# Storing the turned fp16 parts of the adjacency matrix and loading them as they are for the last layer

## The chip, the cores and the metric

One core of one Trainium2 chip runs the whole program. The metric is device time in microseconds (us) of one launch. The kernel before the change takes 728.18 us, the median of three runs (727.69 to 729.91). The profiled execution of the same kernel took 727.12 us; the span that its trace shows, from the first instruction to the last, is 724.8 us.

## The reference, cut to what matters

Four graph layers in a row work on x (2048 x 256) and one dense matrix adj (2048 x 2048, float32). Every layer normalizes x, applies a ReLU, computes a term and adds it to x; the last layer takes x's sign instead of a weighted product:

```python
h = relu(layernorm(x)); x = x + (D^-1/2 adj.T D^-1/2) @ (h @ W0) + b0      # layer 0
h = relu(layernorm(x)); inc = adj + head(adj > 0)                         # layer 1
x = x + (inc @ h) / sum(inc)
h = relu(layernorm(x)); ht = (h @ W2) in 4 heads of 256                    # layer 2
e = leaky_relu(src_i + dst_j) + adj;  x = x + mean_heads(softmax(e) @ ht)
h = relu(layernorm(x)); xw = max(sign(h), 0) @ sign(W3).T                  # layer 3
x = x + relu(adj @ xw)
```

So adj is used four times: transposed in layer 0, as rows in layer 1 (with a small number added to the positive entries), as the additive term of the attention in layer 2, and as it is in layer 3. Since the tensor engine contracts over the partitions, layers 1 to 3 need adj (or a matrix made from it) with the contracted index on the partitions, which is the transposed matrix for rows loaded as they are.

## The kernel before, in words

Rows come in 16 blocks of 128 (NB = 16), a quarter (`q`) is four of them, and every float32 operand of the tensor engine is split into two fp16 parts, a high part (the value rounded) and a low part (what is left). adj times 256 is split while it is loaded; the parts stay on chip for layer 0 and are written once to `nat_dram` (fp16, high and low).

**Turning.** Layers 2 and 3 need the transposed adj. `turn_adj(n)` (SP, L383) loads a 512 x 512 tile of one part from `nat_dram` with a transposing DMA, two DMAs for the two parts, into one of two slots (`turn_l1` for the first four tiles, `turn_l2` for the other twelve). There are 16 tiles, four (`g`) to a quarter. GpSimd's queue then writes the tile to `adjt_dram` as float32: `widen_high(n)` (L545) writes the high part, converted, and `add_low(n)` (L549) adds the low part in memory. SP may turn tile n into its slot again when tile n-2 has been widened (semaphores `wide`).

**SP's queue** does all loads in one written order. During layer 1: `load_rows(t)` (L365) brings block t of adj, 1 MB, for the sign and count on ScalarE (L1003, L1007), which leads to the row that VectorE fills (`fill`, L1346) and that the tensor engine transposes (L699). In that order stand tiles 0 and 1 after the load of block 11, then the loads of blocks 12 to 15, then tiles 2 and 3. Tiles 4 to 15 follow in layer 2, four ahead of each `load_e(q)` (L436): that loads quarter q of `adjt_dram` in four groups of four 256 KB DMAs, each group when its place in `e_in` is free (when VectorE has used it in the last head of the quarter before). ScalarE takes the exponential of it in place (`exp_adj`, L1044).

**Layer 2** has 16 groups (4 quarters x 4 heads) of 16 steps. A step: VectorE makes 128x512 numerators (L1473), ScalarE rounds them to the high part (L1168), VectorE takes the low part (L1480), the tensor engine does 12 matmuls (L835 to L837). Four slots lie between VectorE and the tensor engine. After every group ScalarE scales the head's result (L1098) and GpSimd's queue adds it to x (L586).

**Layer 3** needs the transposed adj in fp16 parts once more, all 16 blocks: the tile `at3` has eight places of 8 KB per partition. The float32 rows are loaded from `adjt_dram` (L458, L463), ScalarE rounds them (`at3_high`, L1156), VectorE takes the low part (`at3_low`, L1528): blocks 0 and 1 in quarters of a block inside heads 2 and 3 of the last quarter, block 2 partly at their end, the others after the heads. The tensor engine does 32 matmuls for each block (L877, L878), the first four blocks partly before `xw` is complete; VectorE adds the result to x (`layer3_out`, L1562) and SP stores it (L472).

Of the kernel before, what the change touches and what calls it, by code (L numbers as in the profile page):

```python
# [28 lines left out]
P = 128  # L29
# [10 lines left out]
def gnn_stack(nc, x_d, adj_d, w0_d, b0_d, w2_d, a2_d, w3_d, out_d):  # L40
# [21 lines left out]
    adjt_dram = nc.dram_tensor("adj_t", (NB, P, N), F32, kind="Internal").ap()  # L62
    u_dram = nc.dram_tensor("u_rows", (NB, HEADS, P), F32, kind="Internal").ap()

    with ExitStack() as ctx:
# [120 lines left out]
        adjt_early = [view(RING3 + 8 * KB * (k + 1), [N], F32) for k in range(2)]  # L186
# [17 lines left out]

        def adjt_slot(i):
            if i < 2:
                return adjt_early[i].rearrange("p (g m) -> p g m", g=QB)
            g = TG * ((i - 2) % 4)
            return e_in[:, :, g:g + TG, :].rearrange("p r j n -> p r (j n)")
# [118 lines left out]
        adjt_in = [sem(f"adjt_in{k}") for k in range(6)]  # L328
        at3_hi_done = sem("at3_hi_done")
        at3_lo_done = sem("at3_lo_done")  # L330
# [12 lines left out]
        def _(sp):  # L343
# [117 lines left out]
            def load_adjt(i):  # L461
                k = (i - 2) % 4
                sp.dma_start(adjt_slot(i), adjt_dram[i].rearrange("p (g m) -> p g m", g=QB)  # L463
                             ).then_inc(adjt_in[k], 16)

            for k in range(4):
                sp.wait_ge(p_done, NQ * HEADS * NB - NB + TG * (k + 1))
                load_adjt(2 + k)
# [125 lines left out]
        def _(pe):  # L594
# [288 lines left out]
            pe.wait_ge(at3_lo_done, 2)  # L883
# [4 lines left out]
            pe.wait_ge(at3_lo_done, 3)  # L888
# [3 lines left out]
            pe.wait_ge(at3_lo_done, 4)  # L892
# [6 lines left out]
            for i in range(4, NB):  # L899
                pe.wait_ge(at3_lo_done, i + 1)  # L900
# [5 lines left out]
        def _(act):  # L906
# [165 lines left out]
            for g in range(TG):  # L1072
                act.wait_ge(wide[g], 16)
            ht_high(0)
# [61 lines left out]
            def at3_high(i, part, parts=4):  # L1136
                k = (4 + i) % 8
                if part == 0:
                    if i < 2:
                        act.wait_ge(adjt_in[4 + i], 16)  # L1140
                        if i == 1:
                            act.wait_ge(at3_lo_done, 1)
                    else:
                        act.wait_ge(adjt_in[(i - 2) % 4], 16 * ((i - 2) // 4 + 1))
                    if i == 2:
                        act.wait_ge(at3_lo_done, 2)
                    if i == 3:
                        act.wait_ge(head_added, 16 * (NQ * HEADS - 1))
                        act.wait_ge(xw_done, 2 * (NQ - 1))
                    if i >= 8:  # L1150
                        act.wait_ge(o_ps, i - 7)
                high = at3[:, k, 0, :, :].rearrange("p (g j) n -> p g (j n)", g=QB)
                source = adjt_slot(i)
                if parts > 1:
                    high, source = high[:, part, :], source[:, part, :]
                ins = nc.scalar.activation(high, source, copy)  # L1156
                if part == parts - 1:
                    ins.then_inc(at3_hi_done, 1)

            def head_high(q, hp, b, first, norms=False, turns=False):  # L1160
                head = 2 * hp + b
                group = q * HEADS + head
                for j in range(EARLY if first else 0, NB):
# [38 lines left out]
            at3_high(3, 0, 1)  # L1202
# [8 lines left out]
            for i in range(4, NB):  # L1211
                at3_high(i, 0, 1)
# [3 lines left out]
        def _(dve):  # L1216
# [246 lines left out]
            for g in range(TG):  # L1463
                dve.wait_ge(wide[g], 16)
            vp_cols = vp_j[:, :, :].rearrange("p t h -> p h t")
# [53 lines left out]
            def at3_low(i, part, parts=4):  # L1519
                k = (4 + i) % 8  # L1520
                if part == 0:
# [75 lines left out]
```

## Time and profile before

| | value |
|---|---|
| median of 3 runs | 728.18 us (727.69 to 729.91) |
| profiled execution | 727.12 us, span of the trace 724.8 us |
| TensorE (PE) busy | 691.0 us, 95% of the span |
| VectorE (DVE) busy | 629.4 us, 87% |
| ScalarE (ACT) busy | 472.4 us, 65% |
| GpSimd (POOL) busy | 135.6 us, 19% |
| share of the 16 DMA engines, SP's queue (q1) | 53.7%, 117.10 MB |
| share of the 16 DMA engines, GpSimd's queue (q0) | 25.4%, 41.42 MB |
| layer 2's products, one step | 12 matmuls |
| granted clock | 0.995 of 2.4 GHz in the mean |

Busy time is the time in which an engine works on at least one instruction; DMA-issuing instructions of SP do not count as busy. A DMA's time "to landing" runs from its issue to the last update of its semaphore. In a stretch where both queues are active the DMA share can be above 1, since it adds the times that packets took. Times within the trace count from the span's start: layer 0 ends near 170, layer 1 near 274, the heads of layer 2 run from about 316 to 662, and layer 3 ends at 722.

### The profile page before, as it was taken

The numbers are of one execution on the slowest core, as the hardware profiler recorded it, in microseconds if no ns is written. First come the engines' busy times: TensorE is split into PE (matmuls) and PEld (weight loads), VectorE is DVE, ScalarE is ACT, GpSimd is POOL, SyncE is SP. The second block draws the span as 40 slices with busy tenths as digits, with TensorE's granted clock in tenths as the row PEclk, the third lists the DMA queues.
The fourth block names the chain that finished last, engine by engine and source line by source line (L and its number), as shares of the span: only waits on it lengthen the run. The fifth ranks groups of instructions, "written<-read, shape, count | busy, mean of one in ns | idle before, by whom it ended". The sixth has DMA issues, their size and how long they took to land.

```text
span 724.8 us, 16131 instructions
## 1 busy us (share of the span) xinstructions
PE 691.0 (95%) x6480; PEld 586.1 (81%) x6480; DVE 629.4 (87%) x1161; ACT 472.4 (65%) x814; POOL 135.6 (19%) x162
## 2 busy tenths in 40 slices
PE   3998999986999999999999999999999999999998
PEld 3676888875888885468888888888888888888887
DVE  6898579688999854799999999989999899998683
ACT  3887153648887624886557867578766778667660
POOL 3962721301223220001210021200121000000000
PEclk9999999998999999999999999999999999999999
DMA  9997999677499887759988779997999831126791
GB/s 337 342 318 238 426 424 309 201 185 219 134 275 277 190 175 234 162 127 243 235 193 235 176 166 257 199 267 161 229 224 228 267 129 30 30 81 188 255 392 46
DMA packets 146457, 159.54 MB, mean 220 GB/s; under 512 B 90896, under 2 KB 103888, under 8 KB 141904
## 3 DMA queue, kind: packets, MB, share of 16 engines
q1 hardware_dynamic: 127328, 117.10, 53.7%
q0 software_dynamic: 19056, 41.42, 25.4%
q8 instruction: 52, 0.85, 0.5%
q14 instruction: 21, 0.17, 0.1%
HBM read 76.15 MB, written 52.46 MB: 177 GB/s over the span
## 4 chain that ended last, share of the span: by engine, by line
PE 60%; DVE 21%; ACT 6%; DMA 4%; issue 4%; SPq 2%; POOL 2%; ACTq 0%; DVEq 0%; POOLq 0%
PE ps L835 11%; PE ps L837 11%; PE ps L836 11%; DVE arena L1473 6%; PE ps L775 6%; DVE arena L1480 5%; PE ps L877 4%; PE ps L878 4%; DVE arena L1346 2%; DMA arena<-in_adj_dram 2%; SPq L383 2%; ACT arena L1003 2%; PE ps L719 2%; PE ps L721 1%; PE ps L720 1%
## 5 line engine op out<-in xcount | busy, mean ns | idle before, releaser
L835 PE MATMUL ps<-arena 128*128 128x257 f16 x1024 | 279.9, 273 | 1.0 <-DVE arena L1480 0.6
L837 PE MATMUL ps<-arena 128*128 128x257 f16 x1024 | 279.4, 273 | 0.0
L836 PE MATMUL ps<-arena 128*128 128x257 f16 x1024 | 279.2, 273 | 0.0
L1168 ACT ACTIVATE arena<-arena 128x512 f16<-128x512 f32 x252 | 158.3, 628 | 93.8 <-PE ps L837 56.3
L1473 DVE SCALAR_TENSOR_TENSOR arena<-arena,w_j 128x512 f32<-128x512 f32 x256 | 190.2, 744 | 0.0
L1480 DVE TENSOR_TENSOR arena<-arena 128x512 f16<-128x512 f32 x256 | 175.7, 687 | 8.1 <-ACT arena L1168 7.8
L835 PEld LDWEIGHTS ps<-arena 128*128 128x128 f16 x1024 | 99.9, 98 | 15.0 <-issue 1.4
L836 PEld LDWEIGHTS ps<-arena 128*128 128x128 f16 x1024 | 100.3, 98 | 12.5
L837 PEld LDWEIGHTS ps<-arena 128*128 128x128 f16 x1024 | 99.8, 97 | 12.9
L719 PE MATMUL ps<-arena 128*128 128x257 f16 x256 | 71.1, 278 | 1.9 <-DVE arena L1298 1.9
L721 PE MATMUL ps<-arena 128*128 128x257 f16 x256 | 70.5, 275 | 0.0
L720 PE MATMUL ps<-arena 128*128 128x256 f16 x256 | 70.1, 274 | 0.0
L670 PE MATMUL ps<-arena 128*128 128x256 f16 x224 | 61.1, 273 | 0.0
L671 PE MATMUL ps<-arena 128*128 128x256 f16 x224 | 61.1, 273 | 0.0
L672 PE MATMUL ps<-arena 128*128 128x256 f16 x224 | 61.1, 273 | 0.0
L877 PE MATMUL ps<-arena 128*128 128x256 f16 x256 | 56.2, 273 | 0.9 <-DVE x L1562 0.9
L878 PE MATMUL ps<-arena 128*128 128x256 f16 x256 | 56.2, 273 | 0.0
L1044 ACT ACTIVATE arena<-arena,amax 128x512 f32<-128x512 f32 x64 | 45.4, 710 | 6.8 <-DMA arena<-adj_t 6.8
L586 POOL DMA_DIRECT2D x<-arena x15 | 14.0, 934 | 185.0 <-ACT arena L1098 185.0
L1528 DVE TENSOR_TENSOR arena<-arena 128x2048 f16<-128x2048 f32 (+1 forms) x22 | 37.4, 1705 | 9.5 <-ACT arena L1156 9.5
L957 ACT ACTIVATE arena<-arena,rstd 128x256 f16<-128x256 f32 x16 | 8.1, 508 | 54.2 <-POOL rstd L520 54.2
L1249 DVE SCALAR_TENSOR_TENSOR arena<-arena 128x1024 f16<-128x1024 f32 x32 | 38.7, 1228 | 5.0 <-ACT arena L912 4.3
(154 smaller groups left out, 1154.9 us busy)
## 6 DMA issues: line engine op xcount, KB each, us to landing
adj_t<-arena POOLq DMA_DIRECT2D x32, 1024.0 KB, 7.9
arena<-in_adj_dram SPq DMA_DIRECT2D x32, 512.0 KB, 6.0
arena<-in_adj_dram SPq DMA_DIRECT2D x16, 1024.0 KB, 5.8
adj_parts<-arena SPq DMA_DIRECT2D x16, 1024.0 KB, 25.7
arena<-adj_t SPq DMA_DIRECT2D x64, 256.0 KB, 4.5
arena<-adj_t SPq DMA_DIRECT2D x16, 1024.0 KB, 6.7
x<-arena POOLq DMA_DIRECT2D x15, 512.0 KB, 5.7
arena<-u_rows SPq DMA_DIRECT2D x4, 1024.0 KB, 14.7
```

The costliest lines, as they stand in the source:

```text
L670: mm(ps[:, bank, 0:D], nat[:, t, 0, j, :], g_hi[:, j, :], start=(j == 0), stop=False)
L719: mm(ps[:, bank, 0:DE], parts[:, 0, j, :], h1_hi[:, j, 0:DE], start=s, stop=False)
L720: mm(ps[:, bank, 0:D], parts[:, 0, j, :], h1_lo[:, j, :], start=False, stop=False)
L721: ins = mm(ps[:, bank, 0:DE], parts[:, 1, j, :], h1_hi[:, j, 0:DE], start=False, stop=e)
L835: mm(ps[:, bank, 0:DE], hi, ht_hi[:, head, j, 0:DE], start=s, stop=False)
L836: mm(ps[:, bank, 0:DE], hi, ht_lo[:, head, j, 0:DE], start=False, stop=False)
L837: ins = mm(ps[:, bank, 0:DE], lo, ht_hi[:, head, j, 0:DE], start=False, stop=e)
L877: mm(ps[:, bank, 0:D], at3[:, k, 0, j, :], xw[:, j, :], start=(j == 0), stop=False)
L878: ins = mm(ps[:, bank, 0:D], at3[:, k, 1, j, :], xw[:, j, :], start=False, stop=(j == NB - 1))
L1168: nc.scalar.activation(p_hi[:, j % 4, :], prob[:, j % 4, :], copy).then_inc(p_hi_done, 1)
L1473: v.scalar_tensor_tensor(prob[:, j % 4, :].rearrange("p (r n) -> p r n", r=QB), u_bc[:, h, q * (QB * P):(q + 1) * (QB * P)].rearrange("p ( ...
L1480: v.tensor_tensor(p_lo[:, j % 4, :], prob[:, j % 4, :], p_hi[:, j % 4, :], ALU.subtract).then_inc(p_lo_done, 1)
```

## The change

Each turned tile, high and low part, is also written to a new DRAM tensor `at16_dram` (fp16, 16 MB) by SP: `store_turned(n)`, one DMA of 1 MB in pieces of 1 KB. Layer 3's blocks are loaded from it straight into `at3`, 1 MB each in rows of 8 KB, and the tensor engine waits on their landing. The loads of float32 rows for layer 3, the 16 roundings on ScalarE and the 16 subtractions on VectorE go, those within the last heads too. A slot is turned again when its tile was both widened and stored; ScalarE and VectorE, before they write where the first four tiles stood, wait for their stores too. GpSimd's code is the same.

```diff
+    at16_dram = nc.dram_tensor("adj_t_parts", (NB, P, 2, N), F16, kind="Internal").ap()
...
             def turn_adj(n):
                 q, g = n // TG, n % TG
                 if n >= 2:
+                    sp.wait_ge(stored[n % 2], 16 * (n // 2))
                     sp.wait_ge(wide[(n - 2) % TG], 16 * ((n - 2) // TG + 1))
...
+            def store_turned(n):
+                q, g = n // TG, n % TG
+                slot = (turn_l1 if q == 0 else turn_l2)[n % 2]
+                sp.wait_ge(turned[n % 2], 32 * (n // 2 + 1))
+                sp.dma_start(at16_dram[QB * q:QB * (q + 1), :, :, TG * P * g:TG * P * (g + 1)
+                                       ].rearrange("r p a m -> p a r m"), slot).then_inc(stored[n % 2], 16)
...
             for n in range(2):
                 sp.wait_ge(inc_in[4 - n], 32)
                 turn_adj(n)
+            for n in range(2):
+                store_turned(n)
             for t in range(12, NB):
                 reload_rows(t)
             for n in range(2, QB):
                 turn_adj(n)
+            for n in range(2, QB):
+                store_turned(n)
...
             sp.wait_ge(ht_ps, 2 * NB)
+            def load_parts(i):
+                k = (4 + i) % 8
+                sp.dma_start(at3[:, k, :, :, :].rearrange("p a j n -> p a (j n)"), at16_dram[i]).then_inc(at3_in[k], 16)
+
             for q in range(1, NQ):
                 for g in range(TG):
                     turn_adj(QB * q + g)
+                    if g >= 1:
+                        store_turned(QB * q + g - 1)
+                store_turned(QB * q + TG - 1)
                 load_e(q)
-            for i in range(2):
-                sp.dma_start(adjt_early[i], adjt_dram[i]).then_inc(adjt_in[4 + i], 16)
...
+            for b in range(2):
+                sp.wait_ge(stored[b], 16 * (NB // 2))
+            for i in range(3):
+                load_parts(i)
+            for h in range(HEADS - 1):
+                sp.wait_ge(p_done, ((NQ - 1) * HEADS + h + 1) * NB)
+                load_parts(QB + h)
+            sp.wait_ge(head_added, 16 * (NQ * HEADS - 1))
+            sp.wait_ge(xw_done, 2 * (NQ - 1))
+            load_parts(3)
+            sp.wait_ge(p_done, NQ * HEADS * NB)
+            load_parts(7)
...
-            for i in range(6, NB):
-                sp.wait_ge(at3_lo_done, i - 3)
-                load_adjt(i)
-                if i >= 8:
-                    store_out(i - 8)
+            for i in range(8, NB):
+                sp.wait_ge(o_ps, i - 7)
+                load_parts(i)
+                store_out(i - 8)
...
             def layer3_products(i, blocks):
                 k, bank = (4 + i) % 8, 4 + i % 4
+                pe.wait_ge(at3_in[k], 16 * (i // 8 + 1))
...
             for g in range(TG):
                 act.wait_ge(wide[g], 16)
+            for b in range(2):
+                act.wait_ge(stored[b], 32)
...
-                    if q == NQ - 1 and head >= 2 and j < 4:
-                        at3_high(head - 2, j)
-                    if q == NQ - 1 and head == HEADS - 1 and j >= 12:
-                        at3_high(2, j - 12)
...
-                        if q == NQ - 1 and h >= 2 and 4 <= j < 8:
-                            at3_low(h - 2, j - 4)
...
-            at3_low(2, 0, 1)
-            at3_low(3, 0, 1)
-            for i in range(4, NB):
-                at3_low(i, 0, 1)
-                layer3_out(i - 4)
-            for t in range(NB - 4, NB):
+            for t in range(NB):
                 layer3_out(t)
```

## Rows read from the trace of the kernel before

**Rows 1.** The page's chain that ended last, by line: share of the span.
```profile
PE ps L835 11%; PE ps L837 11%; PE ps L836 11%; DVE arena L1473 6%; PE ps L775 6%; DVE arena L1480 5%; PE ps L877 4%; PE ps L878 4%; DVE arena L1346 2%; DMA arena<-in_adj_dram 2%; SPq L383 2%; ACT arena L1003 2%; PE ps L719 2%; PE ps L721 1%; PE ps L720 1%
```

**Rows 2.** Groups by line, the removed work: count, busy us, mean ns, idle before.
```profile
L1156 ACT ACTIVATE arena<-arena 128x2048 f16<-128x2048 f32 (+1 forms) x25 | 31.8, 1286 | 10.4 <-DMA arena<-adj_t 10.4
L1528 DVE TENSOR_TENSOR arena<-arena 128x2048 f16<-128x2048 f32 (+1 forms) x22 | 37.4, 1705 | 9.5 <-ACT arena L1156 9.5
```

**Rows 3.** Waits of PE, 600 to 690 us: for whom, total us, times, longest.
```profile
PE ps L877 <- DVE x L1562: 0.9, 1, 0.9
PE ps L853 <- ACT arena L1098: 0.4, 1, 0.4
PE ps L835 <- ACT arena L1168: 0.4, 1, 0.4
```

**Rows 4.** Order of time of SP's queue in layer 1: start us, us, line, DMAs.
```profile
206.38 19.22 SPq L365 DMA_DIRECT2D arena<-in_adj_dram  x4
228.00 16.48 SPq L383 DMA_TRANSPOSE arena<-adj_parts  x4
274.14 9.50 SPq L436 DMA_DIRECT2D arena<-adj_t  x16
```

**Rows 5.** Single issues: tile 1's last transpose, then block 12's load, each to landing.
```profile
L383 SPq DMA_TRANSPOSE arena<-adj_parts x1: 2309/2309/2309, 204.0 to 204.0; - x1
...
DMA to landing us min/median/max: 5.0/5.0/5.0
...
L365 SPq DMA_DIRECT2D arena<-in_adj_dram x1: 581/581/581, 206.4 to 206.4; - x1
...
DMA to landing us min/median/max: 6.2/6.2/6.2
```

**Rows 6.** Order of time behind block 12's landing, on ScalarE, VectorE, PE.
```profile
212.61 1.91 ACT L1003 ACTIVATE arena<-arena 128x2048 f16<-128x2048 f32 x1 [1.18 <-DMA arena<-in_adj_dram]
215.03 0.69 DVE L1352 SCALAR_TENSOR_TENSOR arena<-ps,arena 128x512 f16<-128x512 f32 x1 [1.04 <-ACT arena L992]
218.04 0.33 PE L699 MATMUL ps<-ident,arena 128*128 128x128 f32 x1 [0.29 <-DVE arena L1346]
```

**Rows 7.** Price of 1 MB: four 512 B broadcasts of 1 MB, then four 256 KB loads.
```profile
L448 SPq DMA_DIRECT2D arena<-u_rows x4: 379/3829/7026, 290.8 to 300.9; - x4
...
DMA to landing us min/median/max: 9.5/14.7/16.7
...
L436 SPq DMA_DIRECT2D arena<-adj_t x4: 337/432/436, 382.4 to 383.7; - x4
...
DMA to landing us min/median/max: 3.3/3.9/4.3
```

**Rows 8.** Busy us by stretch: PE, PEld, DVE, ACT, POOL, clock, DMA share, GB/s.
```profile
162.40:168.90 6.50, 0.00 (x0) 0.00 (x0) 5.57 (x10) 6.47 (x5) 1.30 (x3) 0.88 1.01 273
169.00:174.10 5.10, 5.10 (x24) 4.08 (x25) 3.97 (x18) 5.10 (x7) 1.37 (x3) 0.50 0.81 247
174.20:179.00 4.80, 4.80 (x47) 4.39 (x46) 4.23 (x5) 2.81 (x6) 0.00 (x0) 1.00 0.18 29
```

**Rows 9.** Quarter 2's first load_e group, from 468.2 us, and who waited for it.
```profile
L436 SPq DMA_DIRECT2D arena<-adj_t x4: 320/432/452, 468.2 to 469.6; - x4
...
  ACT arena L1044: 2.8, 1
...
DMA to landing us min/median/max: 4.4/8.3/9.3
```

**Rows 10.** Waits of PE, 465 to 580 us; then a stretch as in rows 8.
```profile
PE ps L835 <- DVE arena L1480: 0.6, 2, 0.4
440.00:450.00 10.00, 10.00 (x93) 8.87 (x92) 9.92 (x18) 7.01 (x17) 2.07 (x2) 1.00 1.23 262
```

**Rows 11.** Tile 11's two transposes in SP's queue, 452 to 461 us.
```profile
L383 SPq DMA_TRANSPOSE arena<-adj_parts x2: 2122/2273/2424, 450.2 to 452.7; - x2
...
DMA to landing us min/median/max: 4.7/6.1/7.5
```

More of the change, by code:

```diff
@@ L185, in gnn_stack @@
         turn_l2 = [view(RING3 + off, [2, QB, TG * P], F16) for off in (8 * KB, 16 * KB)]
-        adjt_early = [view(RING3 + 8 * KB * (k + 1), [N], F32) for k in range(2)]
         COUNTS = (1, 2, 9, 10, 11)
@@ L202, in gnn_stack @@
         HT_RING = 7
[L205 to L209, printed above, removed]
         H0_BANK = (0, 1, 6)
@@ L327, in gnn_stack @@
         ba_done = sem("ba_done")
-        adjt_in = [sem(f"adjt_in{k}") for k in range(6)]
-        at3_hi_done = sem("at3_hi_done")
-        at3_lo_done = sem("at3_lo_done")
+        at3_in = [sem(f"at3_in{k}") for k in range(8)]
+        stored = [sem(f"stored{b}") for b in range(2)]
         ba_t_ps = sem("ba_t_ps")
@@ L455, in _ @@
                     turn_adj(QB * q + g)
+                    if g >= 1:
+                        store_turned(QB * q + g - 1)
+                store_turned(QB * q + TG - 1)
                 load_e(q)
-            for i in range(2):
-                sp.dma_start(adjt_early[i], adjt_dram[i]).then_inc(adjt_in[4 + i], 16)
[L461 to L468, printed above, removed]
+            for b in range(2):
[10 more added lines that the diff above has]
+            load_parts(7)
             def store_out(t):
@@ L882, in _ @@
             pe.wait_ge(head_scaled, (NQ * HEADS - 1) * QB)
-            pe.wait_ge(at3_lo_done, 2)
             layer3_products(0, range(NB - QB))
@@ L887, in _ @@
             binary_turn(NQ - 1, 0, 0, ba_tail)
-            pe.wait_ge(at3_lo_done, 3)
             layer3_products(2, range(NB - QB))
@@ L891, in _ @@
             binary_product(NQ - 1, 0, 2, bat_tail)
-            pe.wait_ge(at3_lo_done, 4)
             layer3_products(3, range(NB - 2 * QB))
@@ L899, in _ @@
             for i in range(4, NB):
-                pe.wait_ge(at3_lo_done, i + 1)
                 pe.wait_ge(o_done, i - 3)
@@ L1134, in binary_out @@
                                      ps[:, bank + pair, :], copy, scale=1.0 / ADJ_SCALE).then_inc(xw_done, 1)
[L1136 to L1158, printed above, removed]
             def head_high(q, hp, b, first, norms=False, turns=False):
@@ L1201, in _ @@
                                   turns=(hp == 1 and b == 0))
-            at3_high(3, 0, 1)
             for r in range(QB):
@@ L1210, in _ @@
                 binary_out(NQ - 1, pair)
-            for i in range(4, NB):
-                at3_high(i, 0, 1)
         @block.vector
@@ L1464, in _ @@
                 dve.wait_ge(wide[g], 16)
+            for b in range(2):
+                dve.wait_ge(stored[b], 32)
             vp_cols = vp_j[:, :, :].rearrange("p t h -> p h t")
@@ L1517, in head_inverse @@
                 v.reciprocal(inv_l[:, b, :], inv_l[:, b, :]).then_inc(inv_done, 1)
-            def at3_low(i, part, parts=4):
-                k = (4 + i) % 8
-                if part == 0:
-                    dve.wait_ge(at3_hi_done, i + 1)
-                high = at3[:, k, 0, :, :].rearrange("p (g j) n -> p g (j n)", g=QB)
-                low = at3[:, k, 1, :, :].rearrange("p (g j) n -> p g (j n)", g=QB)
-                source = adjt_slot(i)
-                if parts > 1:
-                    high, low, source = high[:, part, :], low[:, part, :], source[:, part, :]
-                ins = v.tensor_tensor(low, source, high, ALU.subtract)
-                if part == parts - 1:
-                    ins.then_inc(at3_lo_done, 1)
             def quarter(q, first):
@@ L1563, in layer3_out @@
                                        ).then_inc(o_done, 1)
-            at3_low(2, 0, 1)
-            at3_low(3, 0, 1)
-            for i in range(4, NB):
-                at3_low(i, 0, 1)
-                layer3_out(i - 4)
-            for t in range(NB - 4, NB):
+            for t in range(NB):
                 layer3_out(t)
```

## The prediction

> **What bounds the kernel now.** I read the chain of waits first. It is mostly matmuls: lines 835 to 837 alone are a third of the span, and VectorE's two instructions of a step (L1473, L1480) come next [rows 1]. The work that the change removes, the splitting of L1156 and L1528, is not among its largest lines, although it is 31.8 us of ScalarE and 37.4 us of VectorE [rows 2]. So the next view is who made the tensor engine wait where that work stands: between 600 and 690 us, 0.9 + 0.4 + 0.4 us in all [rows 3]. That is what there is to win: the rest of the removed work lies beside matmuls that run without a gap.
>
> Then I read SP's queue, since the change adds to it. In layer 1 its order is on the chain: the load of block 12 is issued at 206.38, right behind the transposes of tiles 0 and 1, and the issues of blocks 13 to 15 follow it until 225.6 [rows 4]. It lands 6.2 us later [rows 5], at 212.6, and ScalarE, which had waited 1.18 us for it, starts at 212.61; VectorE, waiting 1.04 us for ScalarE, follows at 215.03; and the tensor engine, 0.29 us idle, at 218.04 [rows 6]. Each waits for the one before it, so this landing has no slack left.
>
> Last I read the loads of the next quarter (`load_e`). ScalarE waited 2.8 us for the first group of quarter 2 [rows 9], the tensor engine 0.6 us in two waits at the ends of quarters 1 and 2 [rows 10]: the four slots between VectorE and the tensor engine just cover the delay, and any more is the tensor engine's.
>
> **What the change removes.** All 25 instructions of L1156 and 22 of L1528 [rows 2]. The waits that they may cause are the three of rows 3. The 0.9 us (VectorE's addition of block 0 stands behind a subtraction) goes for certain; of the two of 0.4 us in the heads I take both. What is late next there is the tensor engine itself. Gain 1.7 us; bounds 0.9 and 1.7. Loads of layer 3 stay sixteen of 1 MB; eight have a place before the products need them, and the later ones are asked for seven blocks ahead, so I cost them at nothing. If that cover is gone, one late landing costs at most the 6.2 us of a 1 MB load [rows 5].
>
> **What one store costs.** Sixteen DMAs of 1 MB in 1 KB pieces; no row shows such a store. Two kinds of load bound it. Four broadcasts of 1 MB in 512 B pieces: the first is issued at 290.8, and the last at 300.9, landing 14.7 us later (the median; its own landing lies near it), so 24.8 us for four, 6.2 us each. Four loads of 256 KB in 2 KB pieces: the first lands at 382.4 + 3.3, the last at 383.7 + 4.3, so 2.3 us for three, 3.1 us for 1 MB [rows 7]. 1 KB lies between; I take 4 us, and 3.1 and 6.2 as the ends.
>
> The Trainium skill ("DMA: Bandwidth & Descriptors", section Specifications) puts the line rate at 435 GB/s for pieces from 512 B on; an estimate from that page is 2.4 us for a store, and the sum below would be 3 us smaller. The trace disagrees for 512 B, with its 6.2 us [rows 7], so I stay with the rows.
>
> **Layer 1: stores 0 and 1 move block 12's load.** SP's order becomes transposes, wait for tile 0, store 0, wait for tile 1, store 1, and only then the loads of blocks 12 to 15. Waiting in SP's queue holds all four. Tile 1's last transpose is issued at 204.0 and lands 5.0 us later, at 209.0 [rows 5]; store 1 can't be issued before, so block 12's load goes out at 209.7 at the earliest (one issue of 0.58 us behind it [rows 5]), 3.3 us late. That is the lower end, with stores that delay nothing. But the load stands behind 2 MB on the same queue. Of its 6.2 us to landing 3.1 are transfer (as four 256 KB loads take), and I give half of the rest, 1.6, to the way from the last byte to the semaphore. So tile 1's bytes are through at 207.4; two stores take 8 us, to 215.4; the load itself 3.1, to 218.5; the message 1.6, to 220.1; and GpSimd's `widen_high(0)`, which falls into this stretch, takes engines from it, by my estimate 1.2 us of its own 4. It lands at 221.3 instead of 212.6: 8.7 us late. By rows 6 there is no slack, so the tensor engine stops 8.7 us more before block 11's transposes. With 6.2 us a store it would be 13 us, and 16 with all 4 us of GpSimd's: the upper end. None of it comes back: the rest of the layer waits for this engine or for the same chain behind it, shifted alike.
>
> Such a stop has one precedent. The tensor engine did nothing from 162.4 to 168.9; after that the granted clock stood at 0.50 (1.2 of 2.4 GHz), with 24 matmuls in 5.1 us where 47 went in 4.8 us at full clock [rows 8]. At the full rate 24 take 2.5 us, so 2.6 us were lost. A stop of 9 us behind steady work should repeat that: 2.5 us more. Bounds 0 (no fall) and 3.5.
>
> Stores 2 and 3 stand behind the last transposes of the layer, issued from 228.0 to 244.5; the next thing in SP's queue, `load_e`, is at 274.1 [rows 4]. ScalarE's and VectorE's new wait for these four stores comes later still, so 30 us cover it; price nothing, and if the cover were gone, one store's 4 us.
>
> **Layer 2: twelve more stores.** `turn_adj`'s new wait for store n-2 stands beside the wait for the same tile's widening, two DMAs one after the other, and ends before it; nothing for that. But the DMA engines are full: a share of 1.23 at 440 to 450 us [rows 10]. In quarter 1, tile 10's transposes are followed by store 9, tile 11's by store 10, and store 11 waits for tile 11, whose last transpose is issued at 452.7 and lands at about 460.2 [rows 11]. `load_e` is due at 468.2 and now stands behind what is left of stores 10 and 11. Stores 9 and 10 compete with GpSimd's writes on which tile 11 waits, so tile 11 comes some 3 us later, store 11 goes out at 463, and with half of the engines its 4 us take 8, to 471: `load_e`'s first group, last landing at 469.6 + 9.3 = 478.9 [rows 9], is some 3 us later. The reserve is used up [rows 10], so that is the tensor engine's loss. The same arrangement of stores 13 to 15 stands ahead of quarter 3's `load_e`: 3 us again. Quarter 1's own loads landed after 4.3 us at most [rows 7] with no wait behind them; stores 5 to 7 I cost at nothing, the reserve covering one 4 us delay. Together 6 us. Bounds: 0 (the stores are through before 468) and 8 us a boundary (stores 10 and 11 whole ahead of the load), 16.
>
> **The sum**, on the profiled execution's 727.12 us (span 724.8 and 2.3 around it): 727.1 - 1.7 + 8.7 + 2.5 + 6 = 742.6. That execution is 1.1 us below the median shown, so against the median it is 743.7; I say 743.
>
> **Rivals.**
> 1. Only layer 1 pays; layer 2's stores are through before `load_e` is due. For it: between tile 11's landing at 460.2 and 468.2 stand 8 us [rows 9, 11], enough for two stores at full rate. Against: the full engines of rows 10. 727.1 - 1.7 + 8.7 + 2.5 = 736.6, on the median 737.7.
> 2. Cheap stores: 3.1 us or less each, no clock fall, no loss in layer 2. Block 12 is then 3.3 to 6 us late: 727.1 - 1.7 + 3.3 to 6 = 728.7 to 731.4, on the median about 730 to 732.5.
> 3. Heavy stores, 6.2 us: 13 in layer 1, 3 for the clock, 10 to 14 in layer 2: 751.5 to 755.5, on the median 753 to 757.
> 4. Not slower: the splitting gone from the last heads and layer 3 is the whole effect, because block 12's load overtakes. That needs it to land by 214.3, 1.7 us later than now, where SP can't issue it before 209.7: it would have to land in 4.6 us instead of 6.2, through two stores. 725.4 to 727, median 726.5 to 728. Decided by that landing.
>
> The Trainium skill ("DMA: Bandwidth & Descriptors", Queues, rings and completion order) says that descriptors of one queue are taken up in ring order but may finish out of it; by that rule the load's data stand behind both stores', as in my sum; served in another order, the fourth case would come nearer. No row here shows a load behind a store.
>
> **Chances and range.** Forecast (738 to 749) 0.45; only layer 1 (734 to 738) 0.22; cheap stores (729 to 734) 0.15; heavy 0.10; not slower 0.08. The likeliest is 743. From 731 to 754 holds some 85%, with a little of the second and third case left out. A measurement of this kernel can tell 0.3%, 2.2 us, from no change. Faster than 726 takes the fourth case at its best: 0.04; within 0.3% (726 to 730.4) the rest of it and the cheapest stores: 0.07; slower 0.89.
>
> **What would show it.** Right: SP's queue shows stores between tile 1's transposes and block 12's load, which lands near 221; PE idles some 9 us before L699 near 218 and its clock stands at 0.50 after it; the waits of L1044 for `adj_t` grow to some 6 us at both quarters' ends; the three waits of rows 3 are gone. Wrong: block 12 lands by 216; the waits at the quarters' ends stay near 2.8 us; or the tensor engine waits elsewhere, on `at3` loads in layer 3 for instance.

## The result and the profile after

The changed kernel takes 749.1 us (median of 4 runs, 745.98 to 753.64) against 727.93 us (727.41 to 729.91) of the kernel before on the same chip: ratio 1.029, 95% interval 1.023 to 1.035. Slower, as forecast, 6 us beyond the forecast of 743 and inside the range of 731 to 754. The profiled execution is the slowest of the four (753.64 us, span 751.8), so its stages below add up to some 6 us more than the medians differ by (27.0 against 21.2). Every trace shows one execution, and those of runs 3, 5 and 12 below are the fastest of theirs: sizes are compared between traces roughly, and the ratios decide.

First the page of the changed kernel: busy times, the granted clock by slice, SP's queue, one group of instructions.

```profile
PE 701.2 (93%) x6480; PEld 591.0 (79%) x6480; DVE 593.2 (79%) x1139; ACT 442.0 (59%) x789; POOL 137.6 (18%) x162
...
PEclk9999999989989999999999999989999899999999
...
q1 hardware_dynamic: 138592, 133.87, 59.1%
...
L1052 ACT ACTIVATE arena<-arena,amax 128x512 f32<-128x512 f32 x64 | 45.5, 710 | 29.7 <-DMA arena<-adj_t 29.7
```

VectorE lost 36 us of work and ScalarE 30, as the diff says, SP's queue gained 16.8 MB, and the span grew by 27 us. The tensor engine issues the same matmuls and is busy 10 us longer: the clock has low slices it did not have. ScalarE's idle time ahead of `exp_adj` (now L1052) is 29.7 us; it was 6.8. In the chain that ended last DMAs now have 27% of the span; they had 4%.

Where the span grew, from the starts of the same instructions in both traces: layer 0 ends 1.6 us earlier (the diff does not touch it; two executions differ by so much), layer 1 costs 7.8 us, the ends of quarters 0, 1 and 2 cost 6.0, 8.4 and 8.6 us, and the tail, from the last head on, gives 2.2 back. -1.6 + 7.8 + 6.0 + 8.4 + 8.6 - 2.2 = 27.0, the difference of the spans.

**Layer 1.** SP's queue in order of time, to be held against [rows 4]:

```profile
192.98 11.90 SPq L377 DMA_TRANSPOSE arena<-adj_parts  x4
204.93 3.04 SPq L385 DMA_DIRECT2D adj_t_parts<-arena  x2
208.01 22.91 SPq L358 DMA_DIRECT2D arena<-in_adj_dram  x4
233.73 16.03 SPq L377 DMA_TRANSPOSE arena<-adj_parts  x4
```

The two stores stand ahead of block 12's load. Single issues, the stores and then that load, each to landing [rows 5]:

```profile
L385 SPq DMA_DIRECT2D adj_t_parts<-arena x2: 580/638/697, 204.9 to 207.4; - x2
...
DMA to landing us min/median/max: 5.1/5.7/6.2
...
L358 SPq DMA_DIRECT2D arena<-in_adj_dram x1: 738/738/738, 208.0 to 208.0; - x1
...
DMA to landing us min/median/max: 8.9/8.9/8.9
```

It goes out 1.6 us later and takes 8.9 us instead of 6.2: it lands at 216.9, 4.3 us later on the clock of the trace and 5.9 later measured from layer 0's end. The chain behind it on ScalarE and the tensor engine, in order of time [rows 6]:

```profile
216.97 1.91 ACT L1011 ACTIVATE arena<-arena 128x2048 f16<-128x2048 f32 x1 [7.13 <-DMA arena<-in_adj_dram]
...
219.91 0.20 PE L753 MATMUL ps<-wa_hi,arena 128*128 128x8 f16 x2 [3.87 <-ACT arena L991]
...
222.40 0.90 PE L710 MATMUL ps<-ident,arena 128*128 128x128 f32 x3 [2.19 <-DVE arena L1325]
```

The tensor engine's waits of the whole stretch, 205 to 280 us, for whom, total, times, longest, of after and then of before:

```profile
PE ps L753 <- ACT arena L991: 3.9, 1, 3.9
PE ps L710 <- DVE arena L1325: 3.3, 2, 2.2
```

```profile
PE ps L699 <- DVE arena L1346: 1.9, 2, 1.6
```

The waits grew from 1.9 to 7.2 us, 5.3 more. Then the stretches around the stop; columns as in [rows 8]:

```profile
213.00:220.00 7.00, 3.13 (x32) 2.58 (x31) 0.60 (x1) 3.03 (x4) 0.00 (x0) 1.00 1.39 384
220.50:227.20 6.70, 4.80 (x23) 3.83 (x24) 6.14 (x14) 5.23 (x7) 3.82 (x5) 0.50 0.67 174
227.40:234.00 6.60, 6.60 (x68) 6.01 (x67) 5.83 (x9) 4.70 (x9) 0.38 (x2) 1.00 1.25 309
```

After the stop the clock stands at 0.50: 23 matmuls in 4.8 busy us, where at the full clock of the next stretch 23 take 6.60 x 23 / 68 = 2.2. That is some 2.6 us more (an estimate: the two stretches do not hold the same mix of matmuls), and 5.3 + 2.6 = 7.9 agrees with the layer's 7.8.

**Layer 2, the end of quarter 1.** The tensor engine's waits between 380 and 610 us, the stretch of three quarters' ends (0.6 us in the last two before [rows 10], none in the first), and SP's queue in order of time:

```profile
PE ps L846 <- DVE arena L1461: 16.9, 4, 6.5
```

```profile
447.97 7.60 SPq L377 DMA_TRANSPOSE arena<-adj_parts  x2
455.61 0.59 SPq L385 DMA_DIRECT2D adj_t_parts<-arena  x1
469.56 10.70 SPq L377 DMA_TRANSPOSE arena<-adj_parts  x2
480.31 4.96 SPq L385 DMA_DIRECT2D adj_t_parts<-arena  x2
485.37 20.75 SPq L441 DMA_DIRECT2D arena<-adj_t  x16
```

After tile 10's transposes and store 9 SP issues nothing for 13 us. Store 9 by itself, then tile 11's transposes, then the first group of `load_e` [rows 9, 11]:

```profile
L385 SPq DMA_DIRECT2D adj_t_parts<-arena x1: 592/592/592, 455.6 to 455.6; - x1
...
DMA to landing us min/median/max: 13.9/13.9/13.9
...
L377 SPq DMA_TRANSPOSE arena<-adj_parts x2: 2386/5330/8275, 469.6 to 472.0; - x2
...
DMA to landing us min/median/max: 7.9/10.3/12.7
...
L441 SPq DMA_DIRECT2D arena<-adj_t x4: 614/1215/1277, 485.4 to 488.6; - x4
...
  ACT arena L1052: 8.3, 1
...
DMA to landing us min/median/max: 7.6/8.0/8.2
```

SP's waits in that stretch are for tile 9's widening (L374), then for store 9 (L377), then for tile 11's landing (L385). The chain of waits (start, us, what) runs over the last two of them to the load:

```profile
SPq L374 <- DMA adj_t<-arena: 8.6, 1, 8.6
SPq L377 <- DMA adj_t_parts<-arena: 4.7, 1, 4.7
SPq L385 <- DMA arena<-adj_parts: 3.8, 1, 3.8
```

```profile
455.61 13.93 DMA adj_t_parts<-arena
...
471.99 12.69 DMA arena<-adj_parts
...
488.58 7.88 DMA arena<-adj_t
```

Tile 11 may be turned when tile 9 is widened and stored. The widening is through 4.7 us before the store, at 464.8; the store, issued 455.6, lands at 469.5 and is the last. Tile 11 lands at 484.7, store 11 waits for it, and `load_e`, behind store 11 in the same queue, goes out at 485.4, although its place had been free since 480.4 (the end of the VectorE instruction that frees it; 468.2 in the trace before). Measured from that moment, tile 11 lands 12.3 us later than before: 2.4 us from the later widening, 4.8 from the wait for store 9, and 5.1 because its own transposes take 15.1 us from the first issue to the landing instead of 10.0 [rows 11]. The tensor engine then stops 5.83 us (order of time), and the clock falls once more (busy time by stretch): 24 matmuls in 5.1 us, then 58 in 6.2.

```profile
498.60 0.38 PE L846 MATMUL ps<-arena 128*128 128x257 f16 x1 [5.83 <-DVE arena L1461]
```

```profile
497.00:503.70 6.70, 5.10 (x24) 3.60 (x25) 5.94 (x10) 5.92 (x11) 0.95 (x2) 0.50 1.04 204
503.80:510.00 6.20, 6.20 (x58) 5.50 (x57) 4.37 (x7) 3.20 (x6) 0.00 (x0) 1.00 1.04 337
```

The same happens at the other two ends: stores 5 and 13 take 15.2 and 13.8 us to land, `load_e` goes out 3.7 and 6.9 us after its place is free, and the tensor engine is idle 4.4 and 6.5 us. At all three ends SP waits for the store when the widening is done, up to 7.7 us (its waits between 320 and 680 us):

```profile
SPq L377 <- DMA adj_t_parts<-arena: 16.8, 3, 7.7
```

From 610 to 752 us the view of waits lists none for the tensor engine: those of [rows 3] are gone and no load of layer 3 holds it.

### The profile page after: what moved, and what is told of

The parts are those of the page before. It is cut to its first block, busy times and chain, and to the rows that moved or that the text cites. A ratio compares the mean times of both kernels' runs of the same rounds, so it can differ in the third digit from the quotient of the medians.

```text
span 751.8 us, 16107 instructions
## 1 busy us (share of the span) xinstructions
PE 701.2 (93%) x6480; PEld 591.0 (79%) x6480; DVE 593.2 (79%) x1139; ACT 442.0 (59%) x789; POOL 137.6 (18%) x162
## 4 chain that ended last, share of the span: by engine, by line
PE 37%; DMA 27%; DVE 15%; ACT 6%; issue 5%; SPq 5%; POOL 4%; ACTq 0%; POOLq 0%; DVEq 0%
DMA adj_t<-arena 8%; DMA arena<-adj_parts 7%; DMA adj_t_parts<-arena 6%; PE ps L786 5%; PE ps L846 5%; PE ps L848 5%; PE ps L847 5%; DMA arena<-adj_t 4%; PE ps L889 4%; PE ps L890 4%; SPq L377 4%; DVE arena L1325 2%; DVE arena L1461 2%; DVE arena L1454 2%; DVE arena L1228 2%
## 5 line engine op out<-in xcount | busy, mean ns | idle before, releaser
L846 PE MATMUL ps<-arena 128*128 128x257 f16 x1024 | 282.9, 276 | 16.9 <-DVE arena L1461 16.9
L848 PE MATMUL ps<-arena 128*128 128x257 f16 x1024 | 282.4, 276 | 0.0
L847 PE MATMUL ps<-arena 128*128 128x257 f16 x1024 | 282.3, 276 | 0.0
L846 PEld LDWEIGHTS ps<-arena 128*128 128x128 f16 x1024 | 101.0, 99 | 32.1 <-ACT arena L1154 17.9
L848 PEld LDWEIGHTS ps<-arena 128*128 128x128 f16 x1024 | 100.9, 99 | 14.1
L847 PEld LDWEIGHTS ps<-arena 128*128 128x128 f16 x1024 | 101.3, 99 | 13.5
L730 PE MATMUL ps<-arena 128*128 128x257 f16 x256 | 72.5, 283 | 2.0 <-DVE arena L1277 2.0
L732 PE MATMUL ps<-arena 128*128 128x257 f16 x256 | 71.9, 281 | 0.0
L1052 ACT ACTIVATE arena<-arena,amax 128x512 f32<-128x512 f32 x64 | 45.5, 710 | 29.7 <-DMA arena<-adj_t 29.7
L1528 DVE SCALAR_TENSOR_TENSOR x<-ps,x 128x256 f32<-128x256 f32 x16 | 6.8, 424 | 48.8 <-PE ps L890 48.8
L597 POOL DMA_DIRECT2D x<-arena x15 | 16.8, 1117 | 146.5 <-ACT arena L1108 146.5
L786 PE MATMUL ps<-arena 128*128 128x512 f16 x192 | 42.5, 379 | 0.1
```

The lines of the kernel that those rows point to most:

```text
L730: mm(ps[:, bank, 0:DE], parts[:, 0, j, :], h1_hi[:, j, 0:DE], start=s, stop=False)
L732: ins = mm(ps[:, bank, 0:DE], parts[:, 1, j, :], h1_hi[:, j, 0:DE], start=False, stop=e)
L786: ins = mm(ps[:, k % HT_RING, :], h2_t[:, ha * DC + c, t * P:(t + 1) * P], wb[:, c, 512 * half:512 * half + 512], start=(n == 0), stop=(n ...
L846: mm(ps[:, bank, 0:DE], hi, ht_hi[:, head, j, 0:DE], start=s, stop=False)
L847: mm(ps[:, bank, 0:DE], hi, ht_lo[:, head, j, 0:DE], start=False, stop=False)
L848: ins = mm(ps[:, bank, 0:DE], lo, ht_hi[:, head, j, 0:DE], start=False, stop=e)
```

## The experiments

Runs 1 to 4 shared one chip, 5 to 8 a second, 9 to 11 the first again, run 12 had a third; each ratio is against the kernel before on the same chip, with its 95% interval. The medians of the kernel before beside them were 729.47, 729.27, 728.95 and 728.79 us. What a layer costs in a trace is counted as above, from the starts of the same instructions in the trace before.

**1. no_stores: the gain alone.**

```diff
-            for n in range(2):
-                store_turned(n)
...
-                sp.dma_start(at3[:, k, :, :, :].rearrange("p a j n -> p a (j n)"), at16_dram[i]).then_inc(at3_in[k], 16)
+                sp.dma_start(at3[:, k, :, :, :].rearrange("p a j n -> p a (j n)"), nat_dram[i * P:(i + 1) * P]).then_inc(at3_in[k], 16)
...
-                    if g >= 1:
-                        store_turned(QB * q + g - 1)
-                store_turned(QB * q + TG - 1)
```

> The changed kernel without any store of turned tiles and without the waits for them; layer 3's blocks are loaded from the split rows that are in memory already, in the same size and form (so the last layer's numbers are those of adj's rows as split, not turned). It has the gain of the change alone. Theory A (the loss comes from where the stores and their waits stand in SP's queue) and theory B (the loss is the DMA traffic that the stores add) both expect some 726 us, 1.7 to 2.2 less than before, no wait of the tensor engine at the quarters' ends beyond the 0.6 us of before, and none in layer 3. Were the new loads of layer 3 themselves at fault, it would be above 728.

All sixteen stores and every wait for them are left out. 725.13 us, ratio 0.995 (0.993 to 0.997). The removed splitting is worth some 2 us in the tail of the trace and half a per cent of the time (0.3 to 0.7), though it was 69 us of two engines' work. Layer 1, in which nothing is changed here, is 1.7 us longer than in the trace before: differences of that size between two traces say nothing. With the sixteen loads kept and only the stores gone, everything lost above is gone too: the loss belongs to the stores and what waits for them.

**2. layer1_stores: only stores 0 to 3.**

```diff
                 for g in range(TG):
                     turn_adj(QB * q + g)
-                    if g >= 1:
-                        store_turned(QB * q + g - 1)
-                store_turned(QB * q + TG - 1)
...
```

> As the one without stores, but tiles 0 to 3 are stored, in the changed kernel's order (tiles 4 to 15 are not stored, and layer 3 loads the split rows that are in memory). Both theories expect the layer 1 part of the loss and nothing at the quarters' ends: 726 + 6 to 9 = 732 to 735 us, block 12's load landing some 6 us later than before, a stop of the tensor engine of 6 us near 217 and one stretch of clock at 0.50 behind it. If the loss at the quarters' ends also shows, it does not come from the stores of layer 2.

Layer 3 loads what it loads in run 1. 732.83 us, 1.0049 (1.002 to 1.008): 7.7 us above run 1 on the same chip. Layer 1 lost 7.6 us in its trace, and the waits are nearly those of the changed kernel:

```profile
PE ps L708 <- DVE arena L1323: 3.3, 2, 2.2
PE ps L751 <- ACT arena L989: 3.2, 1, 3.2
...
PE ps L844 <- DVE arena L1459: 1.2, 2, 0.9
```

The last row is 380 to 610 us: 1.2 us where the changed kernel has 16.9. So layer 1's loss comes without layer 2's stores.

**3. rows_first: block 12's load ahead of the stores.**

```diff
-            for n in range(2):
-                store_turned(n)
             for t in range(12, NB):
                 reload_rows(t)
+            for n in range(2):
+                store_turned(n)
```

> The changed kernel with one move: the loads of blocks 12 to 15 stand ahead of stores 0 and 1 in SP's queue. Theory A: the whole layer 1 part goes, 8 us, to about 741 us; block 12 lands 6.2 us after its issue as before. Theory B: the same 2 MB are written in the same layer, the loads of blocks 14 and 15 and GpSimd's writes meet them, and half or more of the 8 us stays: 745 us or more.

749.27 us, 1.028 (1.024 to 1.032); the expected 741 was missed, and the time is that of the changed kernel. The load again lands after 6.6 us, at 212.8, and the stop at 217 is gone; yet layer 1 still loses 4.5 us in the trace, later. The waits of GpSimd's queue, 215 to 280 us, show where, and the landing of `widen_high(1)`, 10.3 us before:

```profile
POOL adj_t L560 <- DMA adj_t<-arena: 7.9, 2, 5.6
```

```profile
L556 POOL DMA_DIRECT2D adj_t<-arena x1: 1317/1317/1317, 221.0 to 221.0; - x1
...
DMA to landing us min/median/max: 12.7/12.7/12.7
```

The stores now run beside `widen_high(1)`; `add_low` waits 5.6 us for it in GpSimd's queue (3.2 before), with the row norms behind it that the next rows need. The tensor engine stops 1.4 us at 237 and 2.2 us at 243 (1.6 before). That the stores made `widen_high(1)` slower is likely but not shown by this run: it took 12.7 us in run 11 as well, where no store was issued before 242. Part of the cost had moved, and by time nothing was won.

The end of quarter 2 in this trace, where the order is that of the change, shows something else: `load_e` goes out 0.1 us after its place is free, and the end costs 6.3 us all the same. Stores 14 and 15 are on their way until 578 and 580, and the second group of loads takes up to 14.1 us, where it took up to 9.2 before:

```profile
L385 SPq DMA_DIRECT2D adj_t_parts<-arena x2: 580/586/593, 561.6 to 565.4; - x2
...
DMA to landing us min/median/max: 14.9/15.7/16.5
...
L441 SPq DMA_DIRECT2D arena<-adj_t x4: 320/432/432, 576.8 to 578.1; - x4
...
DMA to landing us min/median/max: 6.9/9.1/14.1
```

So loads that are issued in time can still land late behind stores, which is what the prediction had priced for these ends.

**4. reordered: run 3, and in layer 2 two stores early and two behind `load_e`.**

```diff
                 for g in range(TG):
+                    if g == 2:
+                        store_turned(QB * q)
+                        store_turned(QB * q + 1)
                     turn_adj(QB * q + g)
-                    if g >= 1:
-                        store_turned(QB * q + g - 1)
-                store_turned(QB * q + TG - 1)
                 load_e(q)
+                for g in range(2, TG):
+                    store_turned(QB * q + g)
```

> The changed kernel with all sixteen stores, in another order: blocks 12 to 15 ahead of stores 0 and 1; in each later quarter both first tiles stored before the third is turned (while GpSimd's queue still waits for a group's end), and the last two stored behind the next quarter's loads. No wait is taken out and no byte is saved. Theory A: nearly all of the loss goes, 726 to 730 us. Theory B: the same 16 MB still meet full DMA engines, and it stays above 735 us.

733.81 us, 1.0049 (1.001 to 1.008). Above the 726 to 730 expected: layer 1 costs 5 us (one stop of 4.4 us at 236 to 241; `widen_high(1)`, beside the two stores, takes 15.1 us). The quarters' ends are down from 23 us to 4.

**5. last_after: only the quarter's last store goes behind `load_e`.**

```diff
-                store_turned(QB * q + TG - 1)
                 load_e(q)
+                store_turned(QB * q + TG - 1)
```

> The changed kernel with one move: in each later quarter the last tile's store stands behind the next quarter's loads instead of ahead of them. Theory C (SP's queue: the loads go out late, because SP waits for the last tile ahead of them): the loads are issued when VectorE frees their places, as before, 5 us earlier than in the changed kernel at the end of quarter 1, and of the 6 to 8.6 us a boundary only 1 to 3 stay: 733 to 738 us. Theory D (the loads' own time to landing, among stores and GpSimd's writes): issue comes earlier but the landing stays where it was, 747 us or more.

744.76 us, 1.021 (1.013 to 1.028): the 733 to 738 of theory C were missed. In its trace `load_e` goes out 0.1, 1.2 and 0.1 us after its place is free, and the tensor engine is idle 0.5, 3.2 and 1.7 us there; but that trace is its fastest execution (737.96), and the median is not told apart from the changed kernel's second measurement (run 9). So it is not shown that moving the last store alone gains anything.

**6. second_early: the first two stores ahead of the third tile, all four ahead of `load_e`.**

```diff
+                    if g == 2:
+                        store_turned(QB * q)
+                        store_turned(QB * q + 1)
                     turn_adj(QB * q + g)
-                    if g >= 1:
-                        store_turned(QB * q + g - 1)
-                store_turned(QB * q + TG - 1)
+                for g in range(2, TG):
+                    store_turned(QB * q + g)
                 load_e(q)
```

> The changed kernel with one move: in each later quarter the second tile's store stands ahead of the third tile's transposes, so that it is written while GpSimd's queue waits, and the last tile's transposes no longer wait for it (they wait 15.2, 13.9 and 13.8 us for that store's landing now). The last store still stands ahead of the loads. Theory C: the last tile is turned some 6 to 8 us earlier, SP's wait for it ends before the loads are due, and 1 to 4 us a boundary stay: 734 to 741 us. Theory D: the last two stores still stand ahead of the loads in the same queue: 745 us or more.

739.95 us, 1.014 (1.009 to 1.020), within the 734 to 741 of theory C; the interval still touches that of run 9. All four stores still stand ahead of `load_e`, and it goes out in time all the same (0.1 us); the tensor engine is idle 0.8, 3.5 and 2.3 us, since the loads land late behind the stores: the second group of the middle end takes up to 11.8 us (8.6 before). The difference to the change is that the quarter's second store is issued ahead of its third tile's transposes, not behind them, so that the fourth tile, which waits for that store, is turned earlier.

**7. tiles_whole: the change with stores in pieces of 8 KB instead of 1 KB, loads in 1 KB.**

```diff
-    at16_dram = nc.dram_tensor("adj_t_parts", (NB, P, 2, N), F16, kind="Internal").ap()
+    at16_dram = nc.dram_tensor("adj_t_parts", (NB, P, 2, QB, TG * P), F16, kind="Internal").ap()
...
+                sp.dma_start(at16_dram[n], slot).then_inc(stored[n % 2], 16)
```

> The changed kernel with the same order and waits, but each tile is stored as one piece of 8 KB per partition (the loads of layer 3 read pieces of 1 KB instead, two DMAs a block). If the price of 1 KB pieces is what costs, a store lands earlier by 0.5 to 1 us of its 5 us alone, and the loss shrinks by 2 to 5 us, to 744 to 747. If place and waits in SP's queue cost, it stays within 2 us of the changed kernel, 747 to 751. Should layer 3 wait for its loads, that shows as waits of the tensor engine on them at the end.

740.64 us, 1.018 (1.011 to 1.025): below what either theory gave, but by the ratio not told apart from run 9 (1.021, 1.017 to 1.025). In its trace, with the order of the change untouched, `load_e` goes out in time (0.1 us), stores 5, 9 and 13 land after 10.1, 10.4 and 8.1 us, and the waits at the ends are 7.7 us, not 16.9. That the size of the pieces is part of a store's price is a reading of two traces; the times do not show it, and run 11 gains nothing from the same pieces.

**8. placed: reordered, and stores 0 and 1 wait until tile 1 is widened.**

```diff
             for t in range(12, NB):
                 reload_rows(t)
+            sp.wait_ge(wide[1], 16)
             for n in range(2):
                 store_turned(n)
```

> The reordered kernel with one wait more: stores 0 and 1 go out only when tile 1 is widened, so that they do not meet GpSimd's writes of tiles 0 and 1, on which GpSimd's queue and through it the row norms wait. If that meeting is what kept 4 to 5 us of layer 1's loss in both kernels with the rows first, the stop of 4.4 us near 236 goes and layer 1 loses 0 to 2: 727 to 731 us. If the DMA engines' fill as such is the cause, 733 us or more as the reordered one.

738.91 us, 1.016 (1.008 to 1.024): missed. The stop at 236 is gone; one of 4.6 us stands at 274 to 278, where `widen_high(3)`, beside stores 2 and 3, lands after 14.0 us (9.6 before), and tile 3 itself is turned late, behind stores 0 and 1.

**9. after_again: the changed kernel beside runs 10 and 11.**

> The changed kernel once more, unchanged, beside the next two: 1.02 to 1.03 times the kernel before, some 745 to 752 us. Its three later quarters' ends lose 6 to 9 us each again, and layer 1 some 8.

745.3 us, 1.021 (1.017 to 1.025), as expected. The size of the loss differs between the two measurements, 2.1 and 2.9%; its sign does not.

**10. placed_all: stores 2 and 3 wait for their own widening too.**

```diff
+            for g in range(2, TG):
+                sp.wait_ge(wide[g], 16)
             for n in range(2, QB):
                 store_turned(n)
```

> The placed kernel with one wait more: stores 2 and 3 go out only when tiles 2 and 3 are widened, at about 272 us, shortly ahead of the first loads of layer 2. If the meeting of stores with GpSimd's writes, on which the row norms wait, is what costs in layer 1, the stop of 4.6 us near 274 goes and layer 1 loses 0 to 2 us; with 1 to 2 us at two quarters' ends and the gain of some 2 us the time is 726 to 731 us, a ratio of 0.997 to 1.005. If the fill of the DMA engines costs wherever the stores stand, it stays at 733 or more.

733.99 us, 1.009 (1.006 to 1.012): missed, expected up to 1.005. The stop of 4.6 us stays, at 270 to 275. As in run 8, tiles 2 and 3 stand behind the postponed stores 0 and 1; they land 5 and 7 us later than in run 4, and GpSimd waits for its own writes (its queue, 240 to 282 us):

```profile
POOL adj_t L565 <- DMA adj_t<-arena: 14.4, 2, 8.5
```

**11. placed_all_whole: run 10 with run 7's pieces.**

> The same with each tile stored in pieces of 8 KB and layer 3's loads in pieces of 1 KB. If a cheaper store counts where the engines are full (as the kernel with whole tiles alone showed), another 0 to 2 us go at the quarters' ends: 724 to 730 us, 0.993 to 1.003 times the kernel before; layer 3 shows no wait on its loads, which then take longer. If not, it equals the one before it in this list within 1 us, or loses what layer 3's loads cost.

736.79 us, 1.009 (1.006 to 1.012): no better than run 10. The 724 to 730 of a cheaper store did not come.

**12. layer2_order: layer 1 as in the change, run 4's order in layer 2 alone.**

```diff
+                    if g == 2:
+                        store_turned(QB * q)
+                        store_turned(QB * q + 1)
                     turn_adj(QB * q + g)
-                    if g >= 1:
-                        store_turned(QB * q + g - 1)
-                store_turned(QB * q + TG - 1)
                 load_e(q)
+                for g in range(2, TG):
+                    store_turned(QB * q + g)
```

> The changed kernel with layer 1 left as it is, and layer 2's stores moved alone: the first two tiles of a quarter are stored before its third tile is turned, the last two behind the next quarter's loads; the same sixteen stores, bytes and waits. Theory C (late issue of the loads, from SP's waits): the loads are issued within 0.2 us of the moment when they are due at all three quarters' ends, the tensor engine stops 0 to 2.5 us at each instead of 4.5 to 6.5, and 1.006 to 1.013 times the kernel before, 733 to 738 us: layer 1's 7 to 8 us stay. Theory D (the stores' traffic): the loads are issued in time but land late all the same, and the ratio stays at 1.017 or more, 741 us and up.

736.04 us, 1.010 (1.006 to 1.014), as expected of the theory of late issue: `load_e` goes out 0.1 us after its place is free at all three ends. The waits of the tensor engine, 380 to 610 us and then 205 to 280 us:

```profile
PE ps L848 <- DVE arena L1463: 2.0, 2, 1.4
...
PE ps L755 <- ACT arena L993: 3.7, 1, 3.7
PE ps L712 <- DVE arena L1327: 3.3, 2, 2.2
```

Layer 1's stop is untouched, and the 16.9 us of the quarters' ends are 2.0. This trace is the fastest of seven executions and that of the change the slowest of four, but the times say the same: above run 2, which has no stores in layer 2, the change stood 1.6 to 2.4% and this run stands 0.5%. The store traffic is the same sixteen megabytes; only its order changed. So at the quarters' ends it is the order in SP's queue, not the amount of traffic, that costs most. No order that was tried beats the kernel before.

## Why the prediction was right and where it was wrong

**Gain, 1.7 us forecast.** The trace has 2.2, and run 1 has 0.3 to 0.7% of the time, 2 to 5 us. This was right: the splitting lay beside other work, and layer 3's loads cost nothing.

**Layer 1, 11.2 us forecast.** The trace has 7.8, and run 2 stands 7.7 above run 1. The mechanism is shown by runs 1 to 3: block 12's load behind two stores, ScalarE's wait for it, the stop, the clock at 0.50 behind it. The clock term was right (2.5 forecast, 2.6). The mis-sized term is the store, for which I took 4 us. SP's part came out as worked: the load was issued at 208.0, which is 209.6 on the clock of the trace before, and I had 209.7. But behind the two stores it took 8.9 us to land and not 11.6, so the 8.7 us late are 5.9. Of these the tensor engine lost 5.3.

The 2.4 us for a store that I had estimated from the 435 GB/s of the Trainium skill ("DMA: Bandwidth & Descriptors", Specifications) were nearer than my 4 us in this stretch, where the load lost only 2.7 us behind two stores, part of them done before it was issued; stores 5, 9 and 13 of layer 2, with 13.8 to 15.2 us to landing, are far from it. The Trainium skill's rule that one queue's descriptors are taken up in ring order (the same page, Queues, rings and completion order) agrees with this trace: the load did not overtake, and landed at 216.9, behind store 1 (207.4 + 6.2 = 213.6).

**Layer 2, 6 us forecast, the step that failed.** The trace has 23.0; by the ratios of the change (1.021 to 1.029) above run 2 (1.0049) it is 12 to 18 us. What was wrong, in order of weight:

The step that failed is the sentence "`turn_adj`'s new wait for store n-2 stands beside the wait for the same tile's widening ... and ends before it; nothing for that". The store ended after the widening at all three ends, 4.3 to 7.7 us after it, 4.7 at the end of quarter 1. I had priced a store by transfers with next to no write of GpSimd's beside them, 3.1 to 6.2 us [rows 7], and halved the engines for the last store alone; stores 5, 9 and 13, which ran beside GpSimd's writes, took 13.8 to 15.2 us. The transposes of the last tile, for which I had added nothing, took 5.1 us longer at the end of quarter 1. So the last tile landed 12.3 us later, not the 3 that I had given it, its store went out behind it, and `load_e` stood behind that store. Run 12 shows that this order is the cost: 2.0 us of waits instead of 16.9.

What I did forecast, loads that land late behind stores still on their way, is in the traces too, beside the late issue: it is what the end of quarter 2 in run 3 (6.3 us) and most of what is left at the ends in run 6 show. At 3 us an end it was priced too low.

The end of quarter 0, which I had "at nothing", cost 6 us, not far below the others. I read that its loads had landed after 4.3 us at most [rows 7], which is its first group alone, and took this for a reserve; the same queue with the same last tile stands ahead of them: they go out 3.7 us late, and the first group is complete 11.1 us after its first issue, where it took 5.6.

The clock I had charged once, in layer 1. In this trace each of the three stops of 4.4 to 6.5 us at the quarters' ends was followed by a stretch at 0.50 as well, which cost some 2 us each (16.3 us more of waits make 23.0 us of loss).

That the time came within 6 us of the forecast is in part luck: the errors cancel in part, layer 1 being 3.4 us too high and layer 2 17 too low in this trace.

Rival 1, only layer 1 pays, is what run 2 does by leaving layer 2's stores out: 3.4 us above the kernel before on its chip, where I had 9.5. Rival 2, cheap stores, had the price of a store in layer 1 about right, with block 12 landing 3.3 to 6 us late (it was 5.9), but it had no fall of the clock and no loss in layer 2. Rival 3, heavy stores, comes near this trace in its sum, but it put 13 us into layer 1, where 7.8 were lost, and its 6.2 us a store is neither what layer 1 showed nor what layer 2 did. Rival 4, the load overtaking the stores, is refuted: it lands 5.9 us late.

Open: a place in layer 1 where the stores cost nothing (four were tried; the cost went from the row load to GpSimd's `add_low`), how much of the gain in layer 2 is owed to the last store alone (run 5), how the cost at the ends divides between late issue and late landing, and whether larger pieces make a store cheaper (runs 7 and 11).

## What to carry to other kernels

A DMA added to an in-order queue costs what stands behind it: list the next instructions in that queue and what each waits for, above all where the new one must itself wait for a late producer. Price its landing in the stretch where it will run, from a DMA of the same size among the same neighbours, not from one that runs alone. And work taken from engines that are not the bound is worth only the few waits it causes: 69 us of it gave 2 us in the trace and 4 in the medians (run 1).

## What the runs showed of the hardware

In the changed kernel the same store of 1 MB in 1 KB pieces landed 4.6 to 6.2 us after its issue in layer 1. In layer 2 nine of the twelve took 4.9 to 11.1 us; stores 5, 9 and 13, issued 1 to 2 us behind an `add_low` of GpSimd's, took 13.8 to 15.2. Some of GpSimd's writes were slower beside stores as well: `widen_high(1)`, which took 10.0 to 12.7 us with no store beside it (the kernel before and runs 1, 8, 10 and 11), took 15.1 beside two in run 4, and `widen_high(3)` took 14.0 in run 8 (9.6 before). Which of the neighbours makes the difference is not shown.

A transposing DMA held up the queue that issued it: the second one of the last tile kept SP for 8.3 to 9.6 us at the three quarters' ends of the changed kernel, where the kernel before needed 2.0 to 3.0.

The granted clock fell from 1.00 to 0.50, the lower of its two levels, behind two stops of 3.9 and 2.2 us close together in layer 1 and behind one of 4.4 to 6.5 us at each quarter's end, in stretches of otherwise steady work; each fall cost some 2 to 2.6 us on top of the stop.
